# First attention re-tiled: a unit takes both heads of a pair and 256 queries instead of one head and 512, with transposes in place of diagonals for the maxima

## The reference

```python
q = (_rmsnorm(x @ w_q_a, q_a_ln) @ w_q_b).reshape(b, s, H, DQ)      # 16 heads
ckv = x @ w_kv_a
kv = (_rmsnorm(c_kv, kv_a_ln) @ w_kv_b).reshape(b, s, H, DN + DV)   # latent of 64
q_pe = _apply_rope(q_pe, cos, sin)
scores = jnp.einsum('bqhd,bkhd->bhqk', qf, kf) * scale
scores = jnp.where(mask[None, None], scores, jnp.finfo(scores.dtype).min)   # causal
p = jax.nn.softmax(scores, axis=-1)
o = jnp.einsum('bhqk,bkhd->bqhd', p, v).reshape(b, s, H * DV)
return o @ w_out
```

## Time and profile before

| | |
|---|---|
| median of 3 runs (lowest to highest) | 2014.09 us (2013.54 to 2016.42) |
| the profiled execution's own time | 2015.19 us |
| span of its records | 2013.2 us |
| busy PE, DVE, ACT, POOL | 1776.6, 1515.9, 1271.1, 1003.5 us |
| mean granted clock of TensorE | 0.919 |

### The profile page before, as it was taken

One profiled execution on the slowest core, in us unless ns is written; L12 is line 12 of the kernel. 1 busy time (PEld: TensorE's weight loads), 2 busy tenths in 40 slices (PEclk: granted clock), 3 DMA queues, 4 the chain that ended last, 5 costly groups with the idle time before them and its releaser, 6 DMA issues. The chain is left out here.

```text
span 2013.2 us, 28359 instructions
## 1 busy us (share of the span) xinstructions
PE 1776.6 (88%) x9496; PEld 1022.7 (51%) x9496; DVE 1515.9 (75%) x2366; ACT 1271.1 (63%) x2491; POOL 1003.5 (50%) x892
## 2 busy tenths in 40 slices
PE   4668999999999999999999997565979899999996
PEld 3546655555556555555565553455644344444445
DVE  6765888778888778878878886677565888888716
ACT  1147887788888787778877875111334377777760
POOL 0005989788888888788888987002401000000110
PEclk8788999999999999999999998677976699999998
DMA  3200000000000000000000000111330200110001
GB/s 97 76 9 15 1 1 15 1 1 14 1 1 15 1 6 9 1 14 1 1 6 1 1 1 0 45 45 37 74 74 1 32 1 1 19 16 2 2 1 42
DMA packets 26704, 34.40 MB, mean 17 GB/s; under 512 B 5312, under 2 KB 19648, under 8 KB 26432
## 3 DMA queue, kind: packets, MB, share of 16 engines
q1 hardware_dynamic: 25360, 31.28, 6.6%
q10 hardware_dynamic: 1200, 1.31, 0.2%
HBM read 26.03 MB, written 6.29 MB: 16 GB/s over the span
## 5 line engine op out<-in xcount | busy, mean ns | idle before, releaser
L1192 POOL TENSOR_TENSOR lath_summed<-lath_summed,lath_held 128x512 f32<-128x512 f32 (+3 forms) x528 | 595.7, 1128 | 46.5 <-ACT lath_held L1095 6.6
L1903 ACT ACTIVATE atth_probs<-atth_score 128x512 f32<-128x512 f32 (+3 forms) x640 | 293.4, 542 | 166.7 <-PE atth_score L1822 164.7
L1262 DVE TENSOR_TENSOR lath_held<-lath_held,lath_shift 128x512 f32<-128x512 f32 (+1 forms) x448 | 339.3, 791 | 26.2 <-PE lath_shift L1010 24.8
L1090 ACT ACTIVATE lath_held<-lath_score 128x512 f32<-128x512 f32 (+1 forms) x448 | 293.1, 686 | 83.1 <-issue 31.7
L1862 DVE TENSOR_REDUCE atth_maxima<-atth_slot 128x2 f32<-128x1024 f32 (+3 forms) x288 | 286.4, 1042 | 61.6 <-PE atth_slot L1805 60.6
L1095 ACT ACTIVATE lath_held<-lath_held 128x512 f32<-128x512 f32 (+1 forms) x448 | 303.6, 720 | 27.4 <-DVE lath_held L1262 24.5
L998 PE MATMUL lath_out<-lath_held,lat_latent 128*64 128x512 f32 (+3 forms) x1280 | 312.7, 553 | 6.4 <-ACT lath_held L1095 5.6
L983 PE MATMUL lath_score<-lath_query_hi,lat_key_hi 128*128 128x512 f32 (+3 forms) x640 | 261.8, 409 | 23.0 <-ACT lath_held L1090 21.2
L1750 POOL TENSOR_SCALAR_AFFINE_SELECT atth_probs<-atth_probs 128x512 f32<-128x512 f32 x64 | 40.6, 635 | 445.0 <-ACT atth_probs L1903 445.0
L987 PE MATMUL lath_score<-lath_query_hi,lat_key_lo 128*128 128x512 f32 (+3 forms) x640 | 255.9, 400 | 0.0
L1215 DVE TENSOR_TENSOR lath_largest<-lath_score,lath_largest 128x256 f32<-128x256 f32 (+3 forms) x336 | 221.9, 684 | 22.5 <-PE lath_score L987 20.3
(11 more groups left out here) (346 smaller groups left out, 2973.1 us busy)
## 6 DMA issues: line engine op xcount, KB each, us to landing
att_first_query<-att_scratch SPq DMA_DIRECT2D x12, 256.0 KB, 9.3
atth_query<-att_scratch SPq DMA_DIRECT2D x12, 256.0 KB, 9.1
ffn_a_w<-in_L_ffn_W SPq DMA_DIRECT2D x2, 1024.0 KB
lat_raw_out<-in_L_attn_w_out SPq DMA_DIRECT2D x8, 256.0 KB, 2.7
lat_rope<-in_c_rope_feature SPq DMA_DIRECT2D x1, 2048.0 KB, 10.4
ffn_b_w<-in_L_ffn_W SPq DMA_DIRECT2D x2, 1024.0 KB, 7.1
mix_a_factors<-in_L_ffn_factors SPq DMA_DIRECT2D x8, 256.0 KB, 4.3
att_scratch<-attp_high SPq DMA_DIRECT2D x4, 512.0 KB, 3.2
```

The lines of the kernel that those rows point to most:

```text
L1090: nc.scalar.activation(slot(n)[:, tiles, q0:CH], score_bank[n % 2][:, tiles, q0:CH], ACT.Copy)\
L1192: nc.gpsimd.tensor_tensor(total[:, q0:CH], so_far, slot(n)[:, i, q0:CH], ALU.add).then_inc(s["tiles_summed"], 1)
L1262: nc.vector.tensor_tensor(slot(n)[:, tiles, q0:CH], slot(n)[:, tiles, q0:CH], shift[:, q0:CH].unsqueeze(1).broadcast_to([P, count, CH - q0 ...
L1903: nc.scalar.activation(probs[:, step % PROB_STEPS, h, q0:CH], score_bank[u % 3][:, q0:CH], ACT.Exp, scale=SCALE1)\
```

## The change

A unit becomes (pair, block of 256 queries) with both heads side by side: the 512 columns of a score tile are 256 queries of head 0 and the same of head 1. Block `j` (0 to 7) has j+1 steps: j whole ones and one diagonal, of tiles of 512 and 2x128 columns. There are 288 steps. The chunks come in the order 0, 3, 2, 1, so that the units of a pair have 1, 2, 7, 8, 5, 6, 3 and 4 steps. The maxima are spread by four transposes whose weights are the column `row_max` read 128 times with a step of zero; `L1102` and the constants for it go, and the shift is subtracted. The three query slots hold both heads of a chunk each, the slots of `held` are 12, values are ranked 11 steps behind, and the two halves of `lath_largest` share a third row. A step that waits for a query waits for both heads of its chunk.

```diff
+UNIT = CH // 2
+LATENT_CHUNKS = (0, 3, 2, 1)
-LATENT_UNITS = [(pair, j, h) for pair in range(PAIRS) for j in range(NCH) for h in range(2)]
-LATENT_STEPS = [(u, s) for u, (_, j, _) in enumerate(LATENT_UNITS) for s in range(key_tiles(j) // 2)]
-HELD_STEPS = 14
-SECOND_PASS_AFTER = 12.0
+LATENT_UNITS = [(pair, 2 * c + e) for pair in range(PAIRS) for c in LATENT_CHUNKS for e in range(2)]
+LATENT_STEPS = [(u, s) for u, (_, j) in enumerate(LATENT_UNITS) for s in range(j + 1)]
+HELD_STEPS = 12
+SECOND_PASS_AFTER = 11.0
...
+    return [(slice(0, 2), 0)] if s < LATENT_UNITS[u][1] else [(slice(0, 1), 0), (slice(1, 2), P)]
+def by_head(row, q0):
+    return row.rearrange("p (h q) -> p h q", h=2)[:, :, q0:UNIT]
+def joins_maxima(g):
+    u, s = LATENT_STEPS[g]
+    return s >= 1 and s == LATENT_UNITS[u][1] - 1
...
-        add("tensor", 1.3, due, ("query", u), ("split_low", p), of("low", u - 2), of("whole", u - 1))
-        add("scalar", 1.2, urgent, ("diag", u), ("turn_max_out", u), of("spread", u - 1))
-        add("tensor", 0.35, urgent, ("spread", u), ("diag", u), of("add", FIRST_STEP[u] - 1))
+    for n in range(2 * NCH * PAIRS):
+        due = FIRST_STEP[2 * k] - 7.0 + n % 2
+        add("tensor", 1.3, due, ("query", n), ("split_low", p), of("low", n - 2), of("whole", n - 1))
+        add("tensor", 0.55, urgent, ("spread", u), ("turn_max_out", u), of("add", FIRST_STEP[u] - 1))
...
-        query_hi, query_lo = sb("query_hi", [P, QUERY_SLOTS, CH], F32R), sb("query_lo", [P, QUERY_SLOTS, CH], F32R)
-        largest = sb("largest", [P, 2, 2, CH])
+        query_hi, query_lo = sb("query_hi", [P, QUERY_SLOTS, 2, CH], F32R), sb("query_lo", [P, QUERY_SLOTS, 2, CH], F32R)
+        largest = sb("largest", [P, 3, CH])
...
-                            pe.wait_ge(s["query_lo_done"], u + 1)
+                            pe.wait_ge(s["query_lo_done"], 2 * (u // 2) + 2)
...
-                            q0 = queries_from(kt, j)
+                            q0 = P if kt == 2 * j + 1 else 0
+                            scores = by_head(score_bank[n % 2][:, i, :], q0)
+                            cols = slice((u % 2) * UNIT + q0, (u % 2 + 1) * UNIT)
...
-                            if kt >= TPC * j:
-                                nc.tensor.matmul(scores[:, q0:q0 + P], core.ident_b, core.mask_kq, start=False, stop=False)
+                            if kt >= 2 * j:
+                                nc.tensor.matmul(scores[:, :, 0:P], core.ident_b, core.mask_kq.unsqueeze(1).broadcast_to([P, 2, P]),
+                                                 start=False, stop=False)
...
-                        pe.wait_ge(s["diag_ready"], TPC * (n + 1))
+                        pe.wait_ge(freed(("turn_max", n)), use["turn_max", n] // 2 + 1)
...
-                        nc.tensor.matmul(shift[:], ones_r[:], shift_diag[:].rearrange("p t q -> p (t q)"), start=True, stop=True)\
-                          .then_inc(s["spread_done"], 1)
+                        for i in range(TPC):
+                            last = nc.tensor.transpose(shift[:, i * P:(i + 1) * P], row_max[:, n % 2, i:i + 1].broadcast_to([P, P]), core.ident)
+                        last.then_inc(s["spread_done"], 1)
...
-                        for i in range(TPC):
-                            nc.scalar.activation(shift_diag[:, i], minus_ident[:], ACT.Copy, scale=row_max[:, n % 2, i:i + 1]).then_inc(s["diag_ready"], 1)
```

More of the change, by code:

```diff
@@ L822, in latent_plan @@
[L822 to L825 removed]
+        add("tensor", 0.55, urgent, ("spread", u), ("turn_max_out", u), of("add", FIRST_STEP[u] - 1))
+        add("scalar", 0.6, urgent, ("drain", u), ("values", last), of("fold", u - 1))
+        add("vector", 0.85, urgent, ("fold", u), ("drain", u), of("spread_inverse_out", k - 1))
@@ L826, in latent_plan @@
+        if j % 2:
+            add("tensor", 1.1, urgent, ("sums", k), ("sum", FIRST_STEP[u] - 1), ("sum", last), of("project", k - 1, 1))
+            add("scalar", 0.6, urgent, ("sums_out", k), ("sums", k))
             add("tensor", 0.5, urgent, ("turn_sums", k), ("sums_out", k), of("widen", k - 1))
@@ L834, in latent_plan @@
     for g, (u, s) in enumerate(LATENT_STEPS):
-        p, j, h = LATENT_UNITS[u]
-        widths = [(CH - q0) * (tiles.stop - tiles.start) for tiles, q0 in step_parts(g)]
-        total, late = sum(widths), g + SECOND_PASS_AFTER
-        elementwise = sum(0.1 + w / 890 for w in widths)
-        on_scalar = sum(0.1 + w / 1200 for w in widths)
-        held = g - HELD_STEPS
-        add("tensor", 0.1 + 3 * total / 2250, g, ("scores", g), ("low", u), of("scores", g - 1), of("evac", g - 2))
-        add("scalar", on_scalar, g, ("evac", g), ("max", g), of("values", held), of("sum", held))
@@ L849, in latent_plan @@
-        add("pool", (1.3 if sum_parts(g) == 1 else sum(0.15 + w / 420 for w in widths) if len(widths) > 1 else 2.6), late, ("sum", g), ("exp", g), of("sum", g - 1),
+        p, j = LATENT_UNITS[u]
+        late, held, whole = g + SECOND_PASS_AFTER, g - HELD_STEPS, s < j
+        maxima = 0.0 if whole and s == 0 else 1.22 if whole else 1.1
+        joins = 1.1 if joins_maxima(g) or (j == 1 and s == 1) else 0.0
+        add("tensor", 1.45 if whole else 1.35, g, ("scores", g), ("low", 2 * (u // 2) + 1), of("scores", g - 1), of("evac", g - 2))
@@ new lines, in latent_plan @@
+        add("scalar", 1.05, g, ("evac", g), ("max", g), of("values", held), of("sum", held))
+        add("vector", maxima + joins, g, ("max", g), ("scores", g), of("evac", g - 1), of("max", g - 1), of("turn_max", u - 2) if s == 0 else None)
+        add("vector", 1.22 if whole else 1.1, late - 1.0, ("add", g), ("spread", u), ("evac", g), of("add", g - 1))
+        add("scalar", 1.08, late - 0.6, ("exp", g), ("add", g), of("exp", g - 1))
+        add("tensor", 1.0, late, ("values", g), ("exp", g), of("values", g - 1), of("fold", u - 1) if s == 0 else None)
@@ L850, in latent_plan @@
+        add("pool", (1.3 if whole else 2.35) if s == 0 else 2.65 if whole else 2.1, late, ("sum", g), ("exp", g), of("sum", g - 1),
             of("sums", u // 2 - 2) if s == 0 else None)
```

202 lines of the change are left out of this document (97 added, 105 removed).

## The result

The changed kernel took 1953.45 us (median; 1952.55 to 1966.63), the kernel before, measured beside it, 2015.08: a ratio of 0.972, 95% interval 0.969 to 0.975. The profiled execution took 1954.15 us with a span of 1952.4, so 60.8 us less span than before.

A forecast was written before the change was run, and what follows sets the result against it. TensorE's own stream was taken to set the pace. Work -13.4, end -11.4, start +2, waits and clock -7 made -29.8 us against 2015.2, giving 1985.4, stated as 1985; range 1966 to 2004.

The forecast's parts named there:

- TensorE's work: TensorE's stream in the first attention: fewer pieces of scores and values, dearer shift and sums; -13.4 us, ends -19 and +46.
- The shift: Four zero-step transposes replace one product on TensorE, 0.50 us for 0.35: 9.6 us more; high end 1.4 us each time.
- The end: Behind the stage's last score: GpSimd done 20.1 us after it, not 28.0, and less ending work; -11.4 us, ends -14 and -1.
- The start: Stage's first score waits for two queries and moves 4 to 7.3 us; taken as +2 us, ends -1 and +7.
- Waits and clock in the middle: Without ScalarE's diagonals, TensorE's copy waits near pair starts and the slow clock behind them shrink; -7 us, ends -21 and +10.
- new tight spots: Set against the gain near pair starts: fewer spare slots, small units in succession, values one step nearer to copies; ends +10 us.
- The third: The share taken of the at most -21 us from copy waits and slow clock near pair starts: -7 us.
- C: Rival: all holes near pair starts close, with most of the clock loss and more small waits; 1958 to 1966 us, chance 0.14.
- B: Rival: with two slots fewer, scores wait at the ends of 16 long units; +42 us, about 2035, chance 0.07.
- D: Rival: each of the 64 shifts brings a slow-clock stretch of 1.7 us; +109 us, near 2095, chance 0.01.
- the prediction's 4 us: What a measurement of this kernel was said to tell from no change: 0.2%, 4 us.

The follow-up runs named there:

- b_order: The kernel before with only the chunk order changed, to 0, 3, 2, 1; 1995.54 us, ratio 0.991 to before.
- a_order0123: The changed kernel with the chunk order put back to 0, 1, 2, 3; 2004.99 us, ratio 0.995 to before.
- b_transposes: The kernel before with only the maxima spread by four zero-step transposes in place of ScalarE's 256 diagonals; 1989.14 us, ratio 0.988 to before.
- b_all_but_tiles: The kernel before with transposes, chunk order 0, 3, 2, 1, 12 slots and values 11 steps behind, but the old units; 1973.64 us, ratio 0.984 to before.

## Why the prediction came out too small

The loops as a staircase from before to changed: transposes -26.5, then the order -11.6, then 12 slots +0.4, then the new units -14.1; together -51.8. By the steps of the prediction:

**TensorE's work: -13.4 forecast, -22.8 measured. Mis-sized.** Scores went from 461.9 to 436.6 us, -25.3 and not -19.9. Both kernels had been priced too high from single steps (476.2 and 456.3): at full clock a whole step came to 1.53 us in both (the mean over all such tiles), not 1.58. That nearly cancels in the difference, all but 1.2 us. What stayed in it is the 0.08 us put on each of the 64 diagonal steps for the wider masks, 5.1 us: the masks added nothing that shows, for the new diagonal step came to 1.47 us, and the old tiles of 512 and 256 columns to 1.48. The values gave -5.5 (forecast -4.1). The shift cost +6.8, not +9.6; a transpose with zero-step weights costs what any transpose costs, so the upper end of that bound is dead. The sums cost +0.8 (forecast +1).

**The end: -11.4 forecast, -10.6 measured in holes** (from 17.0 to 6.4), with 3.1 us of slow clock on top that was not in the sum. GpSimd was done 21.5 us behind the last score (forecast 20.1). Right, and b_order (8.4) and a_order0123 (16.3) show that the order makes it.

**The start: right in the trace, under-priced.** The first score came at 169.3 (forecast 165 to 169). The holes ahead of it grew by 5.5 us and the slow clock there by 0.7, where the sum had 2 and 7 as its upper end.

**Waits and clock in the middle: -7 forecast, -21.4 measured. This is the step that failed.** The holes in the middle fell by 9.9 us and the slow clock there by 11.5. The cause was named rightly: ScalarE's diagonals at the pair starts, and the clock behind those holes. The prediction put the most that this could give at -21 (8.9 of waits and 12 of clock), and took a third of it, on the ground that new tight spots would eat the rest. Measured is the whole. The third was a choice that no row stood behind, and that the net sum hits the bound is in part luck, since two errors meet in it. First, the bound was too low on the waits: the diagonals alone were worth 21.0 us of holes in the middle, not 8.9, and 10.9 us of slow clock there (b_transposes). The wait was not confined to pair starts, where it stood at six, not seven. Second, the tight spots did eat, but from another side: the new units took 34.5 us out of the stream (b_all_but_tiles to changed), and 13.6 us came back as holes (11.2 of them in the middle) and 7.0 as slow clock. A reading of this, not tested by itself: with less stream per pair, GpSimd's fixed work stands nearer to TensorE's; GpSimd is busy for 899.4 of 1055 us, where it was 919.7 of 1107.

**The second attention: not in the sum, -10.9 measured.** It is the same code. The forecast treated all stages but the changed one as constant, and two executions of the same kernel have it 8.8 us apart. That part is luck. Without it the change is worth 50 us of span, and the time would be near 1964, still just below the range. For the same reason the prediction's 4 us, as what a measurement can tell from no change, is too small for single executions: those of the kernel before spread over 30 us.

**The rivals.** C was the nearest, in mechanism (all holes near pair starts and most of the clock loss) and in size: its terms add up to -49.4, and -49.9 is what the span lost outside the second attention; its work was too small (-13.4) and its start too good (-1), which nearly cancel. B did not happen at 12 slots: alone they cost the kernel before 16.2 us, with the transposes and the order in place 0.4. D did not happen; the clock near the shifts is 1.00. The Trainium skill (TensorE: Matmul & The Clock Gate, Part 4: PE-mode transpose) says that transposes do not count as activity for the clock; in b_transposes 256 more of them went with 12.6 us less slow clock. So what the prediction drew from the rule, slow stretches at the shifts, is refuted for groups of four that take 0.44 us between products; the rule itself, for transposes without products around them, no run here tests.

**What stays open.** Why the order is worth 18 us to the old units and 44 to the new is seen only as waits for the sums, not derived. That the new units give back part of their stream because GpSimd is near is argued, not shown: no kernel made GpSimd's work shorter by itself. And what decides, between executions, whether the second attention gets its slow stretch was not found; one kernel unmoved does both.

## What to carry to other kernels

A price that stands on both sides of a difference may be off and do little harm (here 0.05 us a step, 1.2 us in all); an allowance added on one side alone stays in it whole (0.08 us a step, 5.1 us). When a bound has been worked out, the share of it that is taken needs a row behind it too. When an engine beside the bottleneck is charged with small work at a hand-over, its removal is worth the holes and the slow clock behind them over the whole stage (here 33.6 us for 81.6 us of ScalarE), at a price in the bottleneck's own stream that is easy to bound (6 to 8 us). A shorter stream can give part of its gain back as new waits (here 20.6 of 34.5 us): look at the busy share of the next engines before you count it all.

## What the runs showed of the hardware

The granted clock fell to its lower level behind no hole of over 0.21 us in the 30 us before: in the second attention, after 80 us with TensorE busy for 79.2, a stretch of 23.9 us at 1.2 GHz appeared or didn't in executions of one kernel, and the second attention was 8.8 us longer with it. In the first attention of the kernel before, it fell behind five of six waits of 1.59 to 1.69 us at pair starts, and not behind the one at 1140. The Trainium skill (TensorE: Matmul & The Clock Gate, Part 1: The HAM clock gate) says that the number of slow products at a kernel's start varies from run to run; these traces show such a variation far from any start, and 0.45% of the time in size.

Weights read with a step of zero cost nothing extra: 64 groups of four such transposes came to 28.0 us, the 64 groups of turned maxima beside them to 31.4.
